# Three of the first four units by Strassen instead of two, with W2's sums made by accumulating DMAs

## Chip, cores and metric

One core of a Trainium2 chip runs the kernel. The metric is the device time in microseconds (us) of one execution. TensorE multiplies, VectorE and ScalarE do the elementwise work, GpSimd (POOL in the profile) a little of it, SyncE (SP) issues nearly all DMAs.

## What is computed

```python
B, N, V_DIM, Q_DIM = (64, 128, 1024, 512)      # x is (64, 128, 1024), all float32
q_emb = relu(cond_1024 @ W3 + b3)              # (64, 1024)
v_sum = sum(x, axis=1, keepdims=True)
y = (N * x + v_sum) * q_emb[:, None, :]
out = x + relu(y @ W2 + b2)                    # W2 is (1024, 1024)
```

Nearly all of the work is `y @ W2`: 8192 rows by 1024 by 1024, in an accuracy close to float32.

## The kernel before

**Units, quarters and the seven products.** Two sequences of `x` make a unit of 256 tokens, so there are 32 units, and two units make a pair: 16 pairs, 0 to 15. A unit is a 2 x 2 matrix of quarters A11, A12, A21, A22. The first index (t in the code) is the sequence, the second (h) the half of the 1024 features. A quarter lies in SBUF as 128 features by 4 tiles by 128 tokens (128 x 512 elements). W2 likewise has the quadrants b11, b12, b21, b22. A plain unit takes eight products of a quarter with a quadrant. By Strassen's method in Winograd's form a unit takes seven, named m = 1 to 7, in the order 1, 5, 6, 2, 7, 3, 4, with the two units c = 0, 1 of a pair alternating. Products 1, 2 and 4 use A11, A12 and A22 as they are, the others use sums of quarters. On W2's side the products use b11, b21, b22 and four sums t1 to t4 (OPERAND, line 54).

**Precision.** Each operand is split into a high part (a cast to fp32r, on ScalarE) and a low part (the difference, on VectorE). A product is 4 feature tiles by 3 matmuls of 512 columns (high by high, high by low, low by high), 12 matmuls into one of the 8 PSUM banks of `acc`. The parts of the tokens go through a ring of 7 places (`a_hi`, `a_lo`); a cast (`cast`, line 393, `cast_first`, 384) waits until the product that last read its place is done, and a product waits for the low part (`low`, 691, `low_first`, 686) by the semaphore `lo_ready`.

**Per unit, around the products.** VectorE sums the tokens (`token_sums`, 615) and makes scale and bias (`scalars`, 618). The tiles are then scaled in place, as a rule by ScalarE (`scale_quarter`, 406, four instructions a quarter), in the head also by VectorE and GpSimd. VectorE makes the sums of quarters (`sum_block`, 658). ScalarE seeds banks with the bias or with product 1 and saves the results of products 6 and 5 to SBUF tiles (`save_u2`, 473, `save_m5`, 464), because product 7 adds onto product 6's bank and product 3 onto product 5's; TensorE waits for these copies (lines 354 to 359). VectorE combines (`c22_sum`, `c12_sum`), applies relu and adds `x` (`result`, 705). SyncE loads and stores; a slot of `x_sb` (four units in all) is loaded again when the low part of the unit's product 4 is made (`load_pair`, 240).

**The head.** Pair 0 is multiplied plainly, 16 products (PLAIN_PRODUCTS, line 41), pair 1 is the first by Strassen (line 368), and a loop does the others (line 370). The token transform needs `q_emb`, so W3 comes first, staged in the `x_sb` slots of pair 1, whose tokens are loaded once its sums are taken (line 224). W2's quadrants are loaded once each, split in pieces (SPLIT, line 46; `cast_w`, `low_w`). The sums t1, t2 and t4 are made by VectorE in `w_stage` (`w_sum`, 702), t3 by GpSimd (line 611); for t4 b21 is loaded a second time (line 234).

**What sets the order.** Every engine has its own list of instructions, written out by hand in the code, and works it strictly in order; semaphores tie the lists together. An instruction whose wait isn't met holds up all that stand behind it on its engine. The lists of the head are lines 490 to 540 (ScalarE), 599 to 611 (GpSimd), 743 to 815 (VectorE) and 206 to 238 (SyncE); those of a pair are `pair` on ScalarE (542) and VectorE (817).

## Time and profile before

| | |
|---|---|
| median of 3 runs | 634.45 us (634.28 to 634.79) |
| the profiled execution | 634.83 us, span 633.0 us |
| TensorE busy | 628.6 us (99%), granted clock 1.00 |
| VectorE busy | 445.5 us (70%) |
| ScalarE busy | 419.0 us (66%) |
| GpSimd busy | 11.4 us (2%) |
| DMA | 108.83 MB, mean 172 GB/s |

The span runs from the first to the last instruction of the profiled execution; about 1.8 us of its time lie outside. Busy times are sums of instruction durations; on VectorE and ScalarE an instruction starts up to 0.1 us before the one ahead of it has ended, so a row's duration is longer than its share of a full list. A "releaser" is the instruction whose semaphore ended a wait.

### The profile page before, as it was taken

The numbers are of one execution on the slowest core, as the hardware profiler recorded it, in microseconds if no ns is written. First come the engines' busy times: TensorE is split into PE (matmuls) and PEld (weight loads), VectorE is DVE, ScalarE is ACT, GpSimd is POOL, SyncE is SP. The second block draws the span as 40 slices with busy tenths as digits, with TensorE's granted clock in tenths as the row PEclk, the third lists the DMA queues.
The fourth block names the chain that finished last, engine by engine and source line by source line (L and its number), as shares of the span: only waits on it lengthen the run. The fifth ranks groups of instructions, "written<-read, shape, count | busy, mean of one in ns | idle before, by whom it ended". The sixth has DMA issues, their size and how long they took to land.

```text
span 633.0 us, 9252 instructions
## 1 busy us (share of the span) xinstructions
PE 628.6 (99%) x2791; PEld 518.7 (82%) x2791; DVE 445.5 (70%) x683; ACT 419.0 (66%) x899; POOL 11.4 (2%) x14
## 2 busy tenths in 40 slices
PE   9999999999999999999999999999999999999997
PEld 6788888888888888888888888888888888888886
DVE  3899979675766757687576776757677576776533
ACT  4988886839476594856839577594856839577320
POOL 2130000000000000000000000000000000000000
PEclk9999999999999999999999999999999999999999
DMA  8925736564353734336354353744346354350703
GB/s 326 404 110 198 264 135 216 185 205 152 141 166 133 263 135 149 121 160 232 133 199 145 142 177 133 251 140 139 138 162 232 133 199 134 145 186 0 249 16 133
DMA packets 26654, 108.83 MB, mean 172 GB/s; under 512 B 2960, under 2 KB 3600, under 8 KB 22800
## 3 DMA queue, kind: packets, MB, share of 16 engines
q1 hardware_dynamic: 26208, 108.41, 48.3%
q10 hardware_dynamic: 432, 0.27, 0.2%
q8 instruction: 5, 0.08, 0.1%
q14 instruction: 9, 0.07, 0.0%
HBM read 75.11 MB, written 33.55 MB: 172 GB/s over the span
## 4 chain that ended last, share of the span: by engine, by line
PE 99%; DVE 0%; issue 0%; DVEq 0%
PE acc L293 99%; PE acc L310 1%; DVE xn L878 0%; DVE warm L743 0%; DVEq L57 0%
## 5 line engine op out<-in xcount | busy, mean ns | idle before, releaser
L293 PE MATMUL acc<-w_hi,a_hi 128*128 128x512 f32 x904 | 352.0, 389 | 0.0
L293 PE MATMUL acc<-w_lo,a_hi 128*128 128x512 f32 x904 | 351.7, 389 | 0.0
L293 PE MATMUL acc<-w_hi,a_lo 128*128 128x512 f32 x904 | 351.7, 389 | 0.0
L409 ACT ACTIVATE x_sb<-x_sb,bias,scale 128x128 f32<-128x128 f32 x492 | 203.2, 486 | 11.6 <-DVE bias L622 11.6
L293 PEld LDWEIGHTS acc<-w_hi,a_hi 128*128 128x128 f32 x904 | 169.7, 188 | 35.9 <-DVE a_lo L683 0.6
L293 PEld LDWEIGHTS acc<-w_hi,a_lo 128*128 128x128 f32 x904 | 169.7, 188 | 35.2
L293 PEld LDWEIGHTS acc<-w_lo,a_hi 128*128 128x128 f32 x904 | 169.7, 188 | 35.0
L694 DVE TENSOR_TENSOR a_lo<-x_sb,a_hi 128x512 fp32r<-128x512 f32 x150 | 103.5, 690 | 106.3 <-ACT a_hi L404 105.6
L404 ACT CAST a_hi<-x_sb 128x512 fp32r<-128x512 f32 x150 | 93.3, 622 | 38.6 <-PE acc L293 37.3
L404 ACT CAST a_hi<-s 128x512 fp32r<-128x512 f32 x60 | 37.4, 623 | 74.3 <-PE acc L293 69.1
L616 DVE TENSOR_REDUCE vsum<-x_sb 128x16 f32<-128x2048 f32 (+1 forms) x38 | 73.6, 1942 | 6.6 <-DMA x_sb<-x_t 6.6
L707 DVE SCALAR_TENSOR_TENSOR xn<-acc,xn 128x512 f32<-128x512 f32 x67 | 45.7, 689 | 32.6 <-PE acc L293 32.6
L462 ACT COPY acc<-acc 128x512 f32<-128x512 f32 x30 | 17.1, 571 | 49.1 <-PE acc L293 49.1
L694 DVE TENSOR_TENSOR a_lo<-s,a_hi 128x512 fp32r<-128x512 f32 x60 | 41.2, 687 | 0.2
L723 DVE TENSOR_TENSOR m_sb<-m_sb,acc 128x512 f32<-128x512 f32 x30 | 20.6, 687 | 23.0 <-PE acc L293 21.6
L733 DVE TENSOR_TENSOR u_sb<-u_sb,acc 128x512 f32<-128x512 f32 x30 | 20.6, 687 | 8.4 <-PE acc L293 8.4
L707 DVE SCALAR_TENSOR_TENSOR xn<-m_sb,xn 128x512 f32<-128x512 f32 x30 | 20.6, 685 | 0.2
L673 DVE TENSOR_TENSOR s<-s,x_sb 128x512 f32<-128x512 f32 x30 | 20.6, 686 | 0.1
L707 DVE SCALAR_TENSOR_TENSOR xn<-u_sb,xn 128x512 f32<-128x512 f32 x30 | 20.5, 685 | 0.1
L669 DVE TENSOR_TENSOR s<-x_sb 128x512 f32<-128x512 f32 x30 | 20.6, 685 | 0.0
L679 DVE TENSOR_TENSOR x_sb<-x_sb,s 128x512 f32<-128x512 f32 x30 | 20.5, 685 | 0.0
L675 DVE TENSOR_TENSOR x_sb<-x_sb 128x512 f32<-128x512 f32 x30 | 20.5, 685 | 0.0
(49 smaller groups left out, 189.3 us busy)
## 6 DMA issues: line engine op xcount, KB each, us to landing
xn<-x SPq DMA_DIRECT2D x64, 512.0 KB, 4.0
out<-xn SPq DMA_DIRECT2D x62, 512.0 KB, 3.3
x_sb<-x_t SPq DMA_DIRECT2D x30, 1024.0 KB, 5.4
x_sb<-w_t SPq DMA_DIRECT2D x4, 512.0 KB, 6.2
x_sb<-x_t SPq DMA_DIRECT2D x4, 512.0 KB, 10.7
u_sb<-w_q SPq DMA_DIRECT2D x3, 512.0 KB, 6.6
m_sb<-w_q SPq DMA_DIRECT2D x3, 512.0 KB, 6.5
out<-xn SPq DMA_DIRECT2D x3, 256.0 KB, 2.9
```

The source lines that it names most:

```text
L293: return nc.tensor.matmul(dst, lhs, rhs, start=False, stop=False, skip_group_check=True)
L404: nc.scalar.copy(a_hi[:, i % RING], operand(m, 2 * parity + c, c)).then_inc(hi_ready, 1)
L409: last = nc.scalar.activation(x_sb[:, slot, h, t, k], x_sb[:, slot, h, t, k], ACT.Identity, bias=bias[:, slot, h, t, k:k + 1], scale=scale ...
L616: nc.vector.tensor_reduce(sums, tokens, AX.X, ALU.add).then_inc(vsum_ready, 1)
L669: last = nc.vector.tensor_tensor(s, a21, a22, ALU.add)
L673: last = nc.vector.tensor_tensor(s, s, a11, ALU.subtract)
L675: last = nc.vector.tensor_tensor(a21, a11, a21, ALU.subtract)
L679: last = nc.vector.tensor_tensor(a12, a12, s, ALU.subtract)
L694: nc.vector.tensor_tensor(a_lo[:, i % RING], operand(m, 2 * parity + c, c), a_hi[:, i % RING].bitcast(fp32), ALU.subtract).then_inc(lo_rea ...
L707: nc.vector.scalar_tensor_tensor(o, bank, 0.0, o, ALU.max, ALU.add).then_inc(ready, 1)
L723: nc.vector.tensor_tensor(m5_sb[:, c], m5_sb[:, c], p_bank(parity, c), ALU.add).then_inc(c22_summed, 1)
L733: nc.vector.tensor_tensor(u2_sb[:, c], u2_sb[:, c], r_bank(c), ALU.add).then_inc(c12_summed, 1)
```

## The change

Only unit 0 is multiplied plainly (8 products). Unit 1 is done by Strassen together with units 2 and 3, 21 products, in one written list FIRST of 29; 14 of them come in a mixed early part, the other 15 in the list LATE. The loop over pairs 2 to 15 stays. In the new text m = 1 to 7 keep their meaning, `late(u, m)` is the place of a late operand among all operands made, and the products below are counted P0 to P28.

```diff
-    MADE = [((0, 0), 0, 4), ((1, 0), 0, 1), ((0, 0), 1, 2), ((1, 0), 1, 0),
-            ((0, 1), 0, 5), ((1, 1), 0, 3), ((0, 1), 1, 6), ((1, 1), 1, 4), ((0, 0), 0, 1)]
...
+    LATE = [(1, 5), (2, 5), (3, 5), (1, 3), (1, 6), (2, 3), (1, 7), (3, 3), (2, 6), (3, 6), (1, 4),
+            (2, 7), (3, 7), (2, 4), (3, 4)]
+    MADE = [(0, A11, 0), (0, A21, 1), (1, A11, 2), (2, A11, 3), (0, A12, 4), (0, A22, 5), (1, A12, 6), (2, A12, 2),
+            (3, A11, 3), (3, A12, 2)]
+    EARLY = len(MADE)
+    MADE += [(u, HOME[m], (j + 6) % RING) for j, (u, m) in enumerate(LATE)]
+    U1_BANK = {1: 0, 6: 0, 7: 0, 4: 0, 2: 5, 5: 1, 3: 1}
...
+    FIRST = [(0, "c11", 0, "b11", 3), (0, "c21", 1, "b11", 6), (1, 1, 2, "b11", 0), (2, 1, 3, "b11", 2),
+             (0, "c11", 4, "b21", 3), (0, "c21", 5, "b21", 6), (1, 2, 6, "b21", 5), (2, 2, 7, "b21", 4),
+             (0, "c12", 0, "b12", 1), (0, "c22", 1, "b12", 7), (3, 1, 8, "b11", 3),
+             (0, "c12", 4, "b22", 1), (0, "c22", 5, "b22", 7), (3, 2, 9, "b21", 5)]
+    FIRST += [(u, m, EARLY + j, OPERAND[m], late_bank(u, m)) for j, (u, m) in enumerate(LATE)]
```

W3 is staged in `xn`, the tile of the untransformed tokens, and the slots of units 2 and 3 are free for early loads. `s12` stays W2's stage throughout the head: the sums of quarters of units 1 to 3 are made in place, in quarters of `x_sb`, for which GpSimd takes A11 - A21 (`s3`) and the later sums and differences change sign.

```diff
-        w3_stage = x_sb[:, 2:4].rearrange("p s h t k n -> p (s h t k n)").rearrange("p (s t n) -> p s t n", s=KT, t=QT)
+        w3_stage = xn[:].rearrange("p c t d -> p (c t d)").rearrange("p (s t n) -> p s t n", s=KT, t=QT)
...
+        m5_u1, u2_u1 = u2_sb[:, 0], u2_sb[:, 1]
```

TensorE's waits for unit 1, and SyncE's loads and stores after the first ones:

```diff
+                if u == 1:
+                    if part == 2:
+                        pe.wait_ge(q_u1_seeded, 1)
+                    if part == 5:
+                        pe.wait_ge(r_u1_seeded, 1)
+                    if part == 3:
+                        pe.wait_ge(m5_u1_saved, 1)
+                    if part == 7:
+                        pe.wait_ge(u2_u1_saved, 1)
+                    if part == 4:
+                        pe.wait_ge(c22_u1_summed, 1)
...
+            sp.wait_ge(lo_ready, 6)
+            load_next(0)
+            store_first(0, 0, (c11_done, c12_done))
+            store_first(0, 1, (c22_done, c21_done))
+            for t in range(2):
+                sp.wait_ge(stored[0][t], 16)
+                load_xn(2, 0, t)
+            store_first(1, 0, (c11_done, c12_done))
+            sp.wait_ge(lo_ready, late(1, 4) + 1)
+            load_next(1)
```

ScalarE's list from the casts of t1 on (before it: `cast_first(4)`, `cast_first(5)`, `seed_q_u1()`, `scale_first(1, A12)`, casts 6 and 7, a seed, b12, two seeds, cast 8, b22, a seed):

```diff
+            for h in range(2):
+                cast_w("t1", h, t1_summed[h])
+            scale_first(3, A12)
+            cast_first(9)
+            scale_first(3, A22)
+            seed_q(1, 1, 1)
+            scale_first(2, A22)
+            cast_first(late(1, 5))
+            for h in range(2):
+                cast_w("t3", h, t3_summed[h])
+            act.wait_ge(b_step_ready, 1)
+            act.wait_ge(c12_done, 1)
+            nc.scalar.copy(acc[:, U1_BANK[5]], b_step[:]).then_inc(r_u1_seeded, 1)
+            act.wait_ge(c21_done, 1)
+            nc.scalar.copy(r_bank(0), b_step[:]).then_inc(r_seeded, 1)
+            cast_first(late(2, 5))
+            cast_w("t2", 0, t2_summed[0])
+            act.wait_ge(c22_done, 1)
+            nc.scalar.copy(r_bank(1), b_step[:]).then_inc(r_seeded, 1)
+            cast_first(late(3, 5))
+            cast_w("t2", 1, t2_summed[1])
+            save_m5_u1()
+            cast_first(late(1, 3))
+            cast_first(late(1, 6))
+            save_m5(1, 0)
+            cast_first(late(2, 3))
+            save_m5(1, 1)
+            cast_first(late(1, 7))
+            scale_usual(2, 0, 0)
+            cast_first(late(3, 3))
+            save_u2_u1()
+            cast_first(late(2, 6))
+            cast_first(late(3, 6))
+            for h in range(2):
+                cast_w("t4", h, t4_summed[h])
+            cast_first(late(1, 4))
+            scale_usual(2, 0, 1)
...
+            cast_first(late(3, 4))
+            save_u2(1, 1, 0)
+            scale_usual(2, 0, 3)
+            save_u2(1, 1, 1)
+            for n in (4, 5):
+                scale_usual(2, 0, n)
```

GpSimd's list. `add_half` is the accumulating DMA: the quadrant comes from HBM once more and is added to what lies in the stage, so t1 = b12 - b11 and its like become sums of the quadrants (the signs are taken up by the combinations).

```diff
+            def add_half(halves, kh, mh, h, summed):
+                half = slice(h * 2 * MH, (h + 1) * 2 * MH)
+                pool.dma_start(halves[h], w2_q[kh, mh, :, half], accum_op=ALU.add).then_inc(summed[h], 16)
...
+            scale_tiles(0, A11, range(2, KH))
+            scale_tiles(0, A21, range(KH // 2))
+            scale_tiles(0, A12, range(KH))
+            scale_tiles(0, A22, range(KH))
+            scale_tiles(2, A12, range(KH))
+            pool.wait_ge(w_lo_ready, split("b21", 1))
+            for h in range(2):
+                add_half(w_halves, 0, 1, h, t1_summed)
+            scale_tiles(3, A11, range(KH))
+            for h in range(2):
+                pool.wait_ge(w_lo_ready, split("b12", h))
+                add_half(v_halves, 1, 1, h, t3_summed)
+            pool.wait_ge(b_seeded, len(SEEDED))
+            nc.gpsimd.tensor_tensor(b_step[:], b_step[:], b_first[:], ALU.add).then_inc(b_step_ready, 1)
+            scale_tiles(1, A21, range(KH))
+            s3(1)
+            scale_tiles(1, A22, range(KH))
+            for h in range(2):
+                pool.wait_ge(w_lo_ready, split("t1", h))
+                add_half(w_halves, 1, 1, h, t2_summed)
+            scale_tiles(2, A21, range(KH))
+            s3(2)
+            scale_tiles(3, A21, range(KH))
+            s3(3)
+            for h in range(2):
+                pool.wait_ge(w_lo_ready, split("t2", h))
+                add_half(w_halves, 1, 0, h, t4_summed)
```

VectorE's list, after the b11 low parts (`stats` is the sums and scalars of one quarter, both quarters of a half for (3, A12)):

```diff
+            low_first(3)
+            low_w("b21", 0)
+            stats(1, A12)
+            low_first(4)
+            low_w("b21", 1)
...
+            first_result(0, "c12", 0, 0, 1, c12_done)
+            stats(2, A22)
+            low_first(late(1, 5))
+            first_result(0, "c21", 0, 1, 0, c21_done)
+            stats(3, A21)
+            sum_first(2, 5)
+            first_result(0, "c22", 0, 1, 1, c22_done)
+            low_first(late(2, 5))
+            sum_first(3, 5)
+            sum_first(1, 6)
+            low_first(late(3, 5))
+            sum_first(1, 3)
+            low_w("t3", 0)
+            low_first(late(1, 3))
+            low_w("t3", 1)
+            low_first(late(1, 6))
+            for h in range(2):
+                low_w("t2", h)
+            sum_first(2, 6)
+            sum_first(2, 3)
+            low_first(late(2, 3))
+            low_first(late(1, 7))
+            sum_first(3, 6)
+            sum_first(3, 3)
+            sums_usual(0, 0, x_loaded[0], 16)
+            scalars_usual(2, 0, 0)
+            low_first(late(3, 3))
+            c12_u1()
+            low_first(late(2, 6))
+            low_first(late(3, 6))
+            c22_u1()
+            for h in range(2):
+                low_w("t4", h)
+            low_first(late(1, 4))
+            low_first(late(2, 7))
+            low_first(late(3, 7))
+            sums_usual(0, 1, x_loaded[1], 16)
+            scalars_usual(2, 0, 1)
+            low_first(late(2, 4))
+            low_first(late(3, 4))
```

## Rows read from the trace of the kernel before

**Rows 1.** Page, part 1: busy us of each engine, share of the span, instructions.
```profile
PE 628.6 (99%) x2791; PEld 518.7 (82%) x2791; DVE 445.5 (70%) x683; ACT 419.0 (66%) x899; POOL 11.4 (2%) x14
```

**Rows 2.** Chain that ended last, in order of time: start us, us, what.
```profile
12.55 617.28 PE acc L293 x2728
```

**Rows 3.** Waits of the whole run: engine, line, releaser: us in total, times, longest.
```profile
PEld acc L293 <- DVE a_lo L683: 0.6, 2, 0.4
```

**Rows 4.** Timeline, TensorE's weight loads: start us, us, what, idle before and releaser.
```profile
17.35 0.19 PEld L293 LDWEIGHTS acc<-w_hi,a_hi 128*128 128x128 f32 x1 [0.43 <-DVE a_lo L683]
25.69 0.19 PEld L293 LDWEIGHTS acc<-w_hi,a_hi 128*128 128x128 f32 x1 [0.19 <-DVE a_lo L683]
```

**Rows 5.** Timeline, VectorE, 23 to 28 and 70 to 73 us.
```profile
23.47 1.23 DVE L699 TENSOR_TENSOR w_lo<-u_sb,w_hi 128x1024 fp32r<-128x1024 f32 x1 [0.74 <-ACT w_hi L437]
...
24.95 0.69 DVE L683 TENSOR_TENSOR a_lo<-x_sb,a_hi 128x512 fp32r<-128x512 f32 x1 [0.24 <-ACT a_hi L391]
25.55 1.22 DVE L699 TENSOR_TENSOR w_lo<-m_sb,w_hi 128x1024 fp32r<-128x1024 f32 x1
26.69 0.68 DVE L616 TENSOR_REDUCE vsum<-x_sb 128x4 f32<-128x512 f32 x1
...
27.48 0.68 DVE L683 TENSOR_TENSOR a_lo<-x_sb,a_hi 128x512 fp32r<-128x512 f32 x1
...
70.58 2.28 DVE L616 TENSOR_REDUCE vsum<-x_sb 128x16 f32<-128x2048 f32 x1
...
72.98 0.69 DVE L675 TENSOR_TENSOR x_sb<-x_sb 128x512 f32<-128x512 f32 x1
```

**Rows 6.** Timeline, ScalarE, at 36 and from 73 to 77 us.
```profile
36.55 2.01 ACT L437 CAST w_hi<-w_stage 128x1024 fp32r<-128x1024 f32 x2
...
73.10 1.65 ACT L409 ACTIVATE x_sb<-x_sb,bias,scale 128x128 f32<-128x128 f32 x4 [1.52 <-DVE bias L622]
74.66 0.57 ACT L479 COPY u_sb<-acc 128x512 f32<-128x512 f32 x1
75.12 0.62 ACT L404 CAST a_hi<-x_sb 128x512 fp32r<-128x512 f32 x1
75.64 1.66 ACT L409 ACTIVATE x_sb<-x_sb,bias,scale 128x128 f32<-128x128 f32 x4
```

**Rows 7.** Timeline, GpSimd, looked at one instruction at a time.
```profile
13.29 1.76 POOL L594 TENSOR_SCALAR x_sb<-x_sb,scale,bias 128x128 f32<-128x128 f32 x1 [0.18 <-DVE bias L622]
15.04 0.87 POOL L594 TENSOR_SCALAR x_sb<-x_sb,scale,bias 128x128 f32<-128x128 f32 x1
20.87 0.45 POOL L594 TENSOR_SCALAR x_sb<-x_sb,scale,bias 128x128 f32<-128x128 f32 x1 [4.96 <-DVE bias L622]
38.56 2.40 POOL L611 TENSOR_TENSOR w_extra<-m_sb,w_extra 128x1024 f32<-128x1024 f32 x1
```

**Rows 8.** Page, part 6, DMA issues: count, KB each, median us to landing.
```profile
x_sb<-x_t SPq DMA_DIRECT2D x30, 1024.0 KB, 5.4
...
s<-w_q SPq DMA_DIRECT2D x1, 512.0 KB, 15.5
```

**Rows 9.** Timeline, VectorE, beside GpSimd's work.
```profile
14.21 1.39 DVE L699 TENSOR_TENSOR w_lo<-w_stage,w_hi 128x512 fp32r<-128x512 f32 x2
...
20.69 0.68 DVE L616 TENSOR_REDUCE vsum<-x_sb 128x4 f32<-128x512 f32 x1
...
22.00 0.73 DVE L683 TENSOR_TENSOR a_lo<-x_sb,a_hi 128x512 fp32r<-128x512 f32 x1 [0.42 <-ACT a_hi L391]
...
40.34 0.65 DVE L620 TENSOR_SCALAR scale<-q_emb 128x16 f32<-128x16 f32 x1
```

**Rows 10.** Timeline, SyncE's queue: the issue of half a W2 quadrant.
```profile
24.73 0.33 SPq L194 DMA_DIRECT2D u_sb<-w_q  x1
```

More of the change, by code:

```diff
@@ L339, in _, with product @@
                 last.then_inc(prod_done, 1)
-            def product(p, parity, i, first=False):
+            for n in range(len(FIRST)):
+                first_product(n)
+            def product(p, parity, i):
                 m, c = ORDER[i]
@@ L366, in product @@
                 last.then_inc(prod_done, 1)
-            for i in range(STEPS):
-                product(1, 1, i, first=True)
             with nc.Fori(0, (PAIRS - 2) // 2, engines=(mybir.EngineType.PE,), hint_back_edge=True) as l:
@@ new lines, in cast_first_part, with cast_first @@
+                nc.scalar.copy(a_hi[:, place, part], quarter(u, q)[:, part]).then_inc((hi_started, hi_ready)[h], 1)
+            def cast_first(o):
+                u, q, place = MADE[o]
+                if o < EARLY:
+                    act.wait_ge(x0_scaled[u, q], 2 if o == 1 else 1)
+                else:
+                    m = LATE[o - EARLY][1]
+                    if m == 4:
+                        act.wait_ge(x0_scaled[u, A22], 1)
+                    elif m == 7:
+                        act.wait_ge(s3_ready, u)
+                    else:
+                        act.wait_ge(sum_ready, FIRST_SUMS.index((u, m)) + 1)
+                old = [n for n, (_, _, other, _, _) in enumerate(FIRST) if other < o and MADE[other][2] == place]
@@ new lines, in scale_tiles, with s3 @@
+                last.then_inc(x0_scaled[u, q], 1)
+            def add_half(halves, kh, mh, h, summed):
+                half = slice(h * 2 * MH, (h + 1) * 2 * MH)
+                pool.dma_start(halves[h], w2_q[kh, mh, :, half], accum_op=ALU.add).then_inc(summed[h], 16)
+            def s3(u):
+                pool.wait_ge(lo_ready, [v == u and q == A11 for v, q, _ in MADE].index(True) + 1)
+                pool.wait_ge(x0_scaled[u, A21], 1)
+                nc.gpsimd.tensor_tensor(quarter(u, A11), quarter(u, A11), quarter(u, A21), ALU.subtract).then_inc(s3_ready, 1)
@@ L678, in sum_block @@
                     dve.wait_ge(sum_ready, summed(p, ORDER.index((6, c))))
-                    last = nc.vector.tensor_tensor(a12, a12, s, ALU.subtract)
+                    last = nc.vector.tensor_tensor(a12, a12, s, ALU.add)
                 last.then_inc(sum_ready, 1)
```

493 lines of the change are left out of this document (258 added, 235 removed), and 3 rows, old and new, of the table PLAIN_PRODUCTS.

## Prediction, made before the changed kernel was run

> **What bounds the kernel now.** I read the busy times first [rows 1]: TensorE works for 99% of the span. The chain that ended last, in order of time [rows 2], is one unbroken piece of its matmuls, 617.28 us from 12.55 to 629.83. So time is gained only by giving it fewer matmuls, and lost wherever it has to wait. Third, the waits [rows 3]: TensorE's weight loads waited for another engine twice, 0.6 us in all, and the timeline gives both [rows 4]: 0.43 at 17.35, before the second product, and 0.19 at 25.69, before the fifth. So the 225 products from 17.35 on take (629.83 - 17.35 - 0.19) / 225 = 2.721 us each. VectorE and ScalarE have average slack (70% and 66%), but what they must deliver before each product in the first 100 us decides here.
>
> **What the change removes.** Before: 16 products for the plain pair and 15 x 14 for the others, 226. After: 8 for unit 0, 7 each for units 1 to 3, 14 x 14 for the rest, 225. One product less: **-2.72 us**. The loop over the later pairs keeps its instructions; signs change between add and subtract on the same tiles, at no cost. W3 moves to the space of the token tile: the four loads keep their queue places, and what follows (token tiles now, unit 2 and 3 before) waited for the same sums. The q-sums, the first product and its operands keep their order. I cost these at nothing.
>
> **What it adds, by product.** P0 to P28 are the new products of units 0 to 3; P_n is due at 17.35 + 2.721 (n - 1) plus the waits so far. Each engine works its list in order, so I add the lists up from rows. Pitches (start to start, back to back): VectorE 0.60 for a 512-element operation, 1.13 for 1024, 0.60 + 0.20 for one quarter's sums and scalars, 2.2 + 0.2 for a whole unit's [rows 5]. ScalarE 1.55 for four scaled tiles, 0.46 for a copy into SBUF, 0.52 for a cast, 0.95 for a W2 cast of 1024 [rows 6]. The receiver starts at the end of the full duration (0.69, 1.65, 0.57, 0.62, 1.05) plus about 0.05.
>
> P4 (due 25.51). Before, the low part of its tokens ran at 24.95. Now the sums of (unit 1, A12) stand between it and the W2 low part that started at 23.47 [rows 5]: 23.47 + 1.13 + 0.80 = 25.40, ready at 26.1. TensorE waits 0.6 instead of 0.19: **+0.4**.
>
> P14 (unit 1, m = 5). P11 ends at 17.35 + 11 x 2.721 + 0.6 = 47.9; VectorE takes its result (0.60), then the sums for (2, A22) (0.80), which release ScalarE's four tiles at 49.65. Behind them are a cast (0.52), two W2 casts for t3 (1.90) and only then the bias seed that P14 waits for (0.58): 49.65 + 1.55 + 0.52 + 1.90 + 0.58 + 0.05 = 54.25, against a due time of 53.35: **+0.9**.
>
> P19 (unit 2, m = 3): by the list that the next part adds up, VectorE makes its sum at 66.1, behind the t2 low parts and another sum. Sum, cast and low part in full are 0.74 + 0.67 + 0.74 with the hand-overs, so 68.3, and P19 is due at 67.9: **+0.4**.
>
> P20 (unit 1, m = 7), the largest term. It adds onto the bank of P18, so it waits until ScalarE has saved P18, and that copy is queued behind four tiles of unit 4 and a cast. The tiles need unit 4's scalars, which VectorE makes after a long list. From the end of P11 (48.1 on VectorE): 18 operations of 512, two sums with scalars, four W2 low parts, one unit's sums: 10.8 + 1.6 + 4.5 + 2.4 = 19.3 us of work. Idle inside it: 2.3 (the low part of P14 waits for the four tiles and the cast above), 1.1 (sum (3, m = 5) waits for GpSimd: scalars at 53.9, four tiles at 0.45, a 512 subtraction at 1.2, half of the 1024 one [rows 7]), and 2.0 in six short round trips to ScalarE. 48.1 + 19.3 + 5.4 = 72.8; then 0.1 + 1.55 + 0.52 + 0.57 + 0.05 gives 75.7. P20 is due at 71.0: **+4.7**. Before, ScalarE waited 1.52 at its like place [rows 6], but the save behind it was ready at 75.2 and its product due at 17.35 + 23 x 2.721 = 79.9.
>
> P26 and P27. Unit 5 cannot be loaded until unit 1 has left its slot. P20 ends at 78.4; VectorE's two operations (1.3), two t4 low parts (2.26) and the low part of (1, m = 4) end at 82.9. The 1 MB load takes 5.4 [rows 8], sums and scalars 2.4, ScalarE's four tiles and the save behind them 2.2: 93.2, and P26 is due at 92.0: **+1.2**. ScalarE then has eight more tiles (3.1) and a cast (0.6), VectorE a low part and the difference that P27 waits for (1.3 + 0.1): 98.1 against 95.9, **+2.2**.
>
> GpSimd. Its 8 scaled tiles become 36, with three 512 subtractions, a bias sum and eight accumulating DMAs in place of two 1024 subtractions. Beside a VectorE reduction (20.69) a tile took 0.45; beside a dense run of operations with both operands in SBUF (the pair at 14.21 is its end) one took 1.76 and the next 0.87, and VectorE's small scalar operation at 40.34 lasted 0.65, until GpSimd's subtraction had ended [rows 7, 9]. Each can hold the other up. On the chain above GpSimd has the four tiles of (3, A21) and one subtraction; of VectorE's work beside them two operations have both operands in SBUF, some 0.6 each. I take **+1.0**; the ends are 0 (all at 0.45) and 5.1 (every tile at 0.87, as at 15.04, and every subtraction at 1.8, lengthened by one 0.60 operation). The Trainium skill, "SBUF — State Buffer", section "Who interferes with whom", has the loser blocked for the full instruction: by that rule the sum would go to the upper end, 646.6, and this trace agrees only in part: the tile of 1.76 waited out more than one operation, but the low part at 22.00, begun beside a tile, took 0.73 against the usual 0.69 [rows 9].
>
> The accumulating DMAs: no row shows one. Issue: bounded by SP's 0.33 for such a half [rows 10] and GpSimd's own 2.40 for a tile of that size [rows 7]; I take 1.0, nearer the row that is an issue. At 0.33 the sum stays, at 2.40 P14 waits 1.0 more. Landing: between 5.4 for 1 MB in a quiet stretch and 15.5 for 512 KB in the crowded start [rows 8]. Up to 8 us all eight are covered (t1 is issued at 30 and needed at 38, t2 at 44 for 55, t3 at 34 for 52, t4 at 64 for 76), so they cost nothing; at 12 they cost 2, at 16 some 12. I take 5, near the quiet row, since most are issued after the crowded start. The Trainium skill, "DMA: Bandwidth & Descriptors", section "Anatomy of one DMA", gives about 2.0 us plus the bytes at 436 GB/s, an estimate of 3.2 us, which would leave the sum as it is. In exchange VectorE loses six 1024 subtractions, 6.8 us, already left out of its lists above.
>
> **Sum.** 0.4 + 0.9 + 0.4 + 4.7 + 1.2 + 2.2 + 1.0 = 10.8 of new waits, less 2.72: +8.1. Against the profiled execution (634.83 around a span of 633.0) 642.9; against the median of 634.45, which lies 0.4 below it, **642.5 us**. From P29 on both engines have their former lists, at 70% and 66% busy [rows 1], so I expect nothing further.
>
> **The rivals.** *The feeding keeps pace* (faster). The only gain is the product, so 634.45 - 2.72 = 631.7. It needs the 5.4 us of VectorE's idle before P20 to be absent, since the work alone would have ScalarE's copy ready at 70.3, and unit 5 landed some 3 us earlier than a 5.4 us load gives. For it: the work does fit. Against it: the 2.3 and 1.1 follow from queue order with durations of 690 and 1650 ns that hardly vary. It turns to a gain below 2.7 us of waits. 12%.
>
> *GpSimd becomes the bound* (slower still). It lies in the contention of [rows 7, 9]: with tiles at 0.87 and subtractions at 1.8 the new waits are 14.9 (P14 2.6, P16 2.6, P19 0.9, P5 0.35, the rest as above) and the time 646.6; if an issue also costs 2.40, P14 alone waits 7 and P15 2.8, and the time is 655. It decides once GpSimd's list from 28 on slips by 4 us, its margin at 45.9 before sum (1, m = 5). For it: 24 tiles from 28 to 56, VectorE's fullest stretch. Against: many VectorE operations there are reductions or read PSUM, and beside a reduction the tile took 0.45. 15%.
>
> *A part of the waits falls away*: loads landing after 3.5 us take out 2, no contention 1: 639.5; I hold this inside the forecast.
>
> **Chances.** Forecast 70% (639 to 646), GpSimd bound 15%, feeding keeps pace 12%, something between that ends within 0.2% (1.3 us, about what a measurement of this kernel can tell from no change) 3%. So faster 0.12, same 0.03, slower 0.85. The range 637 to 649 leaves out the gain and the upper part of the GpSimd case, together under 2 in 10.
>
> **What the profile would show.** Right: one break of 4 to 5 us in TensorE between 70 and 77, released by a copy of ScalarE into the u2 tile; ScalarE's tile group before it waiting for VectorE's scalars; a VectorE reduction waiting 4 to 5 us for the token load near 84; breaks of 1 to 2 us near 93 and 98; 2700 matmuls of 512 float columns instead of 2712, and no waits later. Wrong: TensorE's waits in the first 100 us under 3 us in all, or the greatest one before P14 or P16, released through GpSimd.

## The result, and the profile after it

The changed kernel took **651.28 us** (median of 6 executions, 649.89 to 652.42) against 634.58 us for the kernel before on the same chip: ratio 1.0264, 95% interval 1.0254 to 1.0274. That is 16.7 us slower; 8.1 were forecast, and the value lies 2.3 us above the range. The profiled execution took 652.42 us, with a span of 650.3.

The page of the changed kernel, parts 1 (busy us, share, instructions), 2 (the span in 40 slices: the granted clock in tenths) and 5 (operation, count | busy us, mean ns | idle before it, releaser):

```profile
PE 631.9 (97%) x2779; PEld 519.1 (80%) x2779; DVE 445.7 (69%) x692; ACT 411.4 (63%) x878; POOL 39.8 (6%) x52
...
PEclk9997988999999999999999999999999999999999
...
L354 PE MATMUL acc<-w_hi,a_hi 128*128 128x512 f32 x900 | 353.6, 393 | 13.8 <-issue 10.0
...
L721 POOL TENSOR_SCALAR x_sb<-x_sb,scale,bias 128x128 f32<-128x128 f32 x36 | 29.0, 1045 | 20.9 <-DVE bias L772 20.9
```

Against [rows 1], TensorE has 12 matmuls fewer, and its share fell from 99% to 97%: it stood idle 13.8 us before matmuls of this kind. In slices 4, 6 and 7, all within the first 115 us, its clock was not fully granted. GpSimd's busy time went from 11.4 to 39.8 us; a record of one tile lasted 1045 ns on the mean (records overlap: the 36 tiles kept it busy for 29.0 us, 0.81 each).

The last piece of the chain that ended last (start us, us, what) is unbroken, so no wait came later, as forecast:

```profile
106.50 540.47 PE acc L354 x2376
```

It holds P27 and everything behind it and ends at 646.97; [rows 2] ended at 629.83. So 17.14 us have to be found ahead of 110 us. TensorE's breaks are in its timeline (start us, us, instruction, idle before it and releaser):

```profile
17.04 0.50 PE L354 MATMUL acc<-w_hi,a_hi 128*128 128x512 f32 x1 [0.30 <-DVE a_lo L844]
25.87 0.50 PE L354 MATMUL acc<-w_hi,a_hi 128*128 128x512 f32 x1 [0.35 <-DVE a_lo L844]
50.87 0.50 PE L354 MATMUL acc<-w_hi,a_hi 128*128 128x512 f32 x1 [0.18 <-DVE a_lo L844]
59.47 0.77 PE L354 MATMUL acc<-w_hi,a_hi 128*128 128x512 f32 x1 [5.57 <-issue]
82.09 0.77 PE L354 MATMUL acc<-w_hi,a_hi 128*128 128x512 f32 x1 [4.47 <-issue]
101.57 0.47 PE L354 MATMUL acc<-w_hi,a_hi 128*128 128x512 f32 x1 [0.77 <-ACT u_sb L567]
106.50 0.47 PE L354 MATMUL acc<-w_hi,a_hi 128*128 128x512 f32 x1 [1.97 <-DVE m_sb L913]
```

From 25.87 on these are P4, P13, P14, P20, P26 and P27. P14's break is 5.57 us where 0.9 was forecast. And after long breaks the products themselves are slow: the windows (busy us and matmuls of TensorE, granted clock, DMA share, GB/s) show the clock at its lower level, 1.2 instead of 2.4 GHz:

```profile
50.00:55.00 5.00, 3.73 (x16) 1.00 0.22 20
...
56.00:62.00 6.00, 2.53 (x6) 0.50 0.98 263
62.00:63.00 1.00, 1.00 (x4) 0.63 0.92 262
63.00:68.00 5.00, 5.00 (x24) 1.00 0.61 197
...
80.00:86.00 6.00, 3.91 (x9) 0.50 0.23 90
...
107.00:110.00 3.00, 3.00 (x9) 0.52 1.00 422
```

P14 to P19 took 18.15 us from 59.47 to the end of P19 (82.09 less 4.47) instead of 6 x 2.721 = 16.33: 1.8 lost. In the same way P20 to P25 lost 2.4 (101.57 - 0.77 - 82.09 = 18.71), and the last piece, 198 products, 540.47 - 538.76 = 1.7. Summed: idle 0.35 + 0.18 + 5.57 + 4.47 + 0.77 + 1.97 = 13.3, slow products 5.9, less the product saved (2.72), less 0.3 because P1 starts at 17.04 instead of 17.35, less the 0.19 that the kernel before waited too [rows 4]: 16.0 of 17.14. The other 1.2 is in pieces of 0.2 to 0.3 between the starts printed (P1 to P4, P4 to P13, P13 to P14, P26 to P27), for which the timeline names no wait.

**Behind P14.** GpSimd's timeline:

```profile
31.80 4.35 POOL L721 TENSOR_SCALAR x_sb<-x_sb,scale,bias 128x128 f32<-128x128 f32 x4
35.74 1.25 POOL L727 DMA_DIRECT2D s<-w_q  x1
40.67 0.89 POOL L727 DMA_DIRECT2D w_extra<-w_q  x1 [3.68 <-issue]
41.23 1.64 POOL L748 TENSOR_TENSOR b_step<-b_step,b_first 128x512 f32<-128x512 f32 x1
42.51 6.17 POOL L721 TENSOR_SCALAR x_sb<-x_sb,scale,bias 128x128 f32<-128x128 f32 x4
48.83 1.29 POOL L733 TENSOR_TENSOR x_sb<-x_sb 128x512 f32<-128x512 f32 x1 [0.15 <-POOL x_sb L721]
50.11 2.24 POOL L721 TENSOR_SCALAR x_sb<-x_sb,scale,bias 128x128 f32<-128x128 f32 x4
```

The last line is the four tiles of (1,A22), needed for the sum (1,5). Two things stand out: four tiles took 4.35 and 6.17 us where 1.8 (0.45 each) were forecast, and the fourth accumulating DMA came 3.68 us late with no releaser. VectorE's timeline carries the delay on,

```profile
41.49 1.48 DVE L770 TENSOR_SCALAR scale<-q_emb 128x8 f32<-128x8 f32 x1
...
52.45 0.69 DVE L858 TENSOR_TENSOR x_sb<-x_sb 128x512 f32<-128x512 f32 x1 [1.63 <-POOL x_sb L721]
```

and ScalarE's:

```profile
45.02 1.05 ACT L529 CAST w_hi<-w_stage 128x1024 fp32r<-128x1024 f32 x1 [3.54 <-DMA w_stage<-w_q]
...
54.84 1.65 ACT L502 ACTIVATE x_sb<-x_sb,bias,scale 128x128 f32<-128x128 f32 x4 [4.52 <-DVE bias L772]
...
58.79 0.58 ACT L649 COPY acc<-b_step 128x512 f32<-128x512 f32 x1
```

The sum (1,5) waits for GpSimd; behind it on VectorE stand a result and the scalars of (2,A22), behind those on ScalarE four tiles, a cast, two casts of t3, and then the copy of b_step into P14's bank, ready at 59.37. The second half of t1 was cast at 45.02, though its DMA was issued by 32.4. So there were several candidates: the gap on GpSimd, its slow tiles, the late t1, and the order of ScalarE's list. The experiments separate them.

**Behind P20** the profile agrees with the forecast chain, ScalarE's timeline:

```profile
79.36 1.65 ACT L502 ACTIVATE x_sb<-x_sb,bias,scale 128x128 f32<-128x128 f32 x4 [4.56 <-DVE bias L772]
80.91 0.60 ACT L488 CAST a_hi<-x_sb 128x512 fp32r<-128x512 f32 x1
81.42 0.58 ACT L581 COPY u_sb<-acc 128x512 f32<-128x512 f32 x1
```

### The profile page after: what moved, and what is told of

It is laid out like the page before. It is cut to its first block, busy times and chain, and to the rows that moved or that the text cites. A ratio compares the mean times of both kernels' runs of the same rounds, so it can differ in the third digit from the quotient of the medians.

```text
span 650.3 us, 9176 instructions
## 1 busy us (share of the span) xinstructions
PE 631.9 (97%) x2779; PEld 519.1 (80%) x2779; DVE 445.7 (69%) x692; ACT 411.4 (63%) x878; POOL 39.8 (6%) x52
## 4 chain that ended last, share of the span: by engine, by line
PE 87%; POOL 3%; DVE 3%; DMA 2%; ACT 2%; issue 2%; SPq 0%; DVEq 0%; ACTq 0%; POOLq 0%
PE acc L354 87%; POOL x_sb L721 2%; DMA w_stage<-w_q 1%; ACT x_sb L502 1%; DMA x_sb<-x_t 1%; DVE w_lo L877 1%; DVE vsum L766 1%; DVE a_lo L844 0%; ACT a_hi L488 0%; ACT w_hi L529 0%; POOL w_stage L727 0%; SPq L231 0%; DVE xn L882 0%; POOL b_step L748 0%; POOL x_sb L733 0%
## 5 line engine op out<-in xcount | busy, mean ns | idle before, releaser
L354 PE MATMUL acc<-w_hi,a_hi 128*128 128x512 f32 x900 | 353.6, 393 | 13.8 <-issue 10.0
L354 PEld LDWEIGHTS acc<-w_hi,a_hi 128*128 128x128 f32 x900 | 170.2, 189 | 52.4 <-issue 12.2
L502 ACT ACTIVATE x_sb<-x_sb,bias,scale 128x128 f32<-128x128 f32 x468 | 193.3, 486 | 22.6 <-DVE bias L772 22.6
L872 DVE TENSOR_TENSOR a_lo<-x_sb,a_hi 128x512 fp32r<-128x512 f32 x140 | 96.7, 690 | 105.9 <-ACT a_hi L497 105.4
L497 ACT CAST a_hi<-x_sb 128x512 fp32r<-128x512 f32 x140 | 87.1, 622 | 37.6 <-PE acc L354 36.1
L766 DVE TENSOR_REDUCE vsum<-x_sb 128x16 f32<-128x2048 f32 (+2 forms) x43 | 74.4, 1733 | 10.9 <-DMA x_sb<-x_t 10.9
L497 ACT CAST a_hi<-s 128x512 fp32r<-128x512 f32 x56 | 34.8, 622 | 72.8 <-PE acc L354 69.1
L872 DVE TENSOR_TENSOR a_lo<-s,a_hi 128x512 fp32r<-128x512 f32 x56 | 38.5, 688 | 0.4
L721 POOL TENSOR_SCALAR x_sb<-x_sb,scale,bias 128x128 f32<-128x128 f32 x36 | 29.0, 1045 | 20.9 <-DVE bias L772 20.9
L923 DVE TENSOR_TENSOR u_sb<-acc,u_sb 128x512 f32<-128x512 f32 x30 | 20.7, 691 | 8.4 <-PE acc L354 8.4
L844 DVE TENSOR_TENSOR a_lo<-x_sb,a_hi 128x512 fp32r<-128x512 f32 (+2 forms) x26 | 17.5, 685 | 9.0 <-ACT a_hi L488 8.6
L488 ACT CAST a_hi<-x_sb 128x512 fp32r<-128x512 f32 x24 | 14.4, 618 | 12.7 <-DVE x_sb L866 5.5
L567 ACT COPY u_sb<-acc 128x512 f32<-128x512 f32 x30 | 17.4, 580 | 5.4 <-PE acc L354 5.3
## 6 DMA issues: line engine op xcount, KB each, us to landing
x_sb<-x_t SPq DMA_DIRECT2D x7, 512.0 KB, 11.4
```

The lines of the kernel that those rows point to most:

```text
L354: return nc.tensor.matmul(dst, lhs, rhs, start=False, stop=False, skip_group_check=True)
L497: nc.scalar.copy(a_hi[:, i % RING], operand(m, 2 * parity + c, c)).then_inc(hi_ready, 1)
L502: last = nc.scalar.activation(x_sb[:, slot, h, t, k], x_sb[:, slot, h, t, k], ACT.Identity, bias=bias[:, slot, h, t, k:k + 1], scale=scale ...
L567: nc.scalar.copy(u2_sb[:, c], p_bank(parity, c)).then_inc(u2_saved, 1)
L721: last = nc.gpsimd.tensor_scalar(x_sb[:, u, h, t, k], x_sb[:, u, h, t, k], scale[:, u, h, t, k:k + 1], bias[:, u, h, t, k:k + 1], ALU.mult ...
L766: nc.vector.tensor_reduce(sums, tokens, AX.X, ALU.add).then_inc(vsum_ready, 1)
```

## The experiments

Each was timed beside the kernel before, whose medians were 634.0 to 634.8 us. Times are medians; "less" and "more" are against the change's 651.28 or the run named. Runs 1 to 4, 5 to 8, 9 to 11 and 12 are four groups, each with its own timing of the kernel before, so a small difference between groups is judged by the ratios.

**1. The descriptor space of GpSimd's DMAs.**

```diff
-    nc = bacc.Bacc("TRN2", target_bir_lowering=False, num_devices=1, dynamic_dma_scratch_size=1024)
+    nc = bacc.Bacc("TRN2", target_bir_lowering=False, num_devices=1, dynamic_dma_scratch_size=2048)
```

```profile
36.36 1.60 POOL L727 DMA_DIRECT2D w_extra<-w_q  x1
36.92 2.36 POOL L748 TENSOR_TENSOR b_step<-b_step,b_first 128x512 f32<-128x512 f32 x1
```

The gap before the fourth DMA is gone, and with it the wait of the sum (1,5) for GpSimd (it ran at 49.52). P14 came at 56.60 after 3.17 us instead of 5.57. So the stall was one of descriptor space; 3.2 us of P14's wait have another cause. Its tiles stayed slow (four took 4.37 and four 5.78).

**2. Unit 1's eight tiles from GpSimd to ScalarE**, with the small descriptor space.

```diff
-            scale_tiles(1, A21, range(KH))
             s3(1)
-            scale_tiles(1, A22, range(KH))
...
+            scale_first(1, A21)
             act.wait_ge(c11_done, 1)
             nc.scalar.copy(p_bank(1, 1), b_first[:]).then_inc(p_seeded, 1)
-            for h in range(2):
-                cast_w("t1", h, t1_summed[h])
+            cast_w("t1", 0, t1_summed[0])
+            scale_first(1, A22)
+            cast_w("t1", 1, t1_summed[1])
```

> The eight scaled tiles of unit 1's A21 and A22 go from GpSimd to ScalarE (beside the casts of t1), nothing else. Theory A, GpSimd's list is what holds P14: VectorE's wait before sum (1, m = 5) goes (1.6), its two small scalar operations of 1.48 and 1.17 shrink to about 0.2, and the wait before P14 falls from 5.9 to 2 to 4; if it falls below some 2.5 the half clock after it goes as well (1.7 more). The time falls by 2 to 5. Rival C, P14 is held by the late landing of t1's second half (ScalarE waits until 45.0 for it): VectorE's low part of t1 stays at 46 to 48.4 and the time falls by 1.6 at most.

Measured: 648.98 us, ratio 1.0234 (1.0217 to 1.0251); P14 at 57.05 after 3.63. Another way round the same late link, with the same result as 1: the sum (1,5) no longer waits for GpSimd, and over 3 us stay. GpSimd still touches the path: of VectorE's two small operations, expected at 0.2, one fell from 1.17 to 0.15 us, the other grew from 1.48 to 2.35, over an addition and a subtraction of GpSimd.

**3. The save that P20 waits for, ahead of unit 4's tiles.**

```diff
-            scale_usual(2, 0, 0)
             cast_first(late(3, 3))
             save_u2_u1()
+            scale_usual(2, 0, 0)
```

> On ScalarE the four scaled tiles of unit 4 go behind the save of P18 and the cast before it, nothing else. The forecast's step: P20's wait of 4.6 is the queue order; it falls to under 1, the half clock after it (82 to 86.7, worth 2.3) goes too, and the waits before P26 and P27 stay as they are. The time falls by 5 to 7. Rival: VectorE's list is late in any case, so that P21 or P22 takes over the wait and the time falls by less than 2.

Measured: 645.65 us, ratio 1.0172 (1.0152 to 1.0191), 5.6 less than the change by moving one line. P20 has no break any more, the clock stays at 1.00 from 64 to 100 us, and P26 gave back 1.3 (2.05 instead of 0.77). No work was taken away.

**4. The clock.** Matmuls of zeros, 22 ahead of P14 and 18 ahead of P20, fill the idle time. They add onto bank 2 and so change no value.

```diff
             for n in range(len(FIRST)):
+                for _ in range({14: 22, 20: 18}.get(n, 0)):
+                    keep_warm()
                 first_product(n)
```

> TensorE gets 22 matmuls of 512 columns of zeros (bf16, added onto bank 2) before P14 and 18 before P20, where it waits 5.9 and 4.6 us; they change no value. If the half clock after these two waits follows from the idleness: it goes in both places, the time falls by some 4 us (1.7 and 2.3), and the waits end where they ended. Rival: the clock falls for another reason (the work of the head as such): it falls as before and the time stays within 0.5 us, or gets longer by the part of the filling that does not fit.

Measured: 648.47 us, ratio 1.022 (1.0203 to 1.0237), 2.8 less. The windows show the clock whole up to 100 us:

```profile
50.00:60.00 10.00, 9.12 (x41) 1.00 0.66 140
60.00:70.00 10.00, 9.70 (x43) 1.00 0.51 176
...
80.00:90.00 10.00, 9.39 (x42) 1.00 0.13 52
```

P20 still started at 81.86 (82.09 in the change): the 1.8 us that P14 to P19 could have gained went into new waits for VectorE's low parts (0.30 at P16, 0.67 at P19), pieces for which the timeline names no wait, and P20's own gap (4.67 us from the end of P19, filling included, instead of 4.47). Only the clock after P20 was worth something at the end, about its 2.4 us. So the clock's fall is a consequence of TensorE's idleness, and a real cost only where no later wait swallows it.

**5. Both edits, 1 and 3**, with no other line changed, as the base of what follows.

> The 2048-byte scratch and the later tiles of unit 4 together. If the two causes are independent: P14's wait near 3.2 as with the scratch alone, none before P20, and the gains add (2.5 and 5.6): about 643. Rival, they overlap, because what P14 gives back is waited for again behind VectorE's list before P20: about 645.

Measured: 643.63 us, ratio 1.0139 (1.012 to 1.0158). TensorE's timeline:

```profile
56.89 0.47 PE L354 MATMUL acc<-w_hi,a_hi 128*128 128x512 f32 x1 [3.08 <-issue]
75.58 0.47 PE L354 MATMUL acc<-w_hi,a_hi 128*128 128x512 f32 x1 [0.46 <-issue]
94.19 0.47 PE L354 MATMUL acc<-w_hi,a_hi 128*128 128x512 f32 x1 [2.01 <-ACT u_sb L567]
99.13 0.69 PE L354 MATMUL acc<-w_hi,a_hi 128*128 128x512 f32 x1 [1.93 <-DVE m_sb L913]
```

P14, P20, P26, P27. The two edits nearly add up: 2.5 + 5.6 = 8.1 against 7.65 measured.

**6. Unit 4's load later**, on 5, so that it does not cross the accumulating DMAs of t1.

```diff
-            sp.wait_ge(lo_ready, 6)
+            sp.wait_ge(lo_ready, 10)
             load_next(0)
```

> As the run before, and SyncE issues the 1 MB load of unit 4 (not needed before 72) some 20 us later, out of the crowded stretch in which t1 is fetched. Theory D, t1's second half lands late because the DMA queues are crowded: it lands 2 us or more earlier than at 44.8, ScalarE's wait of 2.5 before its cast goes, P14's wait falls by 1 to 2. Rival: the accumulating DMA is slow by itself; the landing stays within 0.5.

Measured: 643.72 us, ratio 1.0137 (1.0114 to 1.0161). The cast of t1's second half came at 43.46 instead of 44.84, so the transfers do hold one another up. But P14 stayed at 57.11 after 3.01. VectorE's timeline tells why: it is back to back from 37.44 to 52.4, whenever t1 lands (three of its lines, and the cast ahead of the first on ScalarE):

```profile
36.79 0.62 ACT L488 CAST a_hi<-x_sb 128x512 fp32r<-128x512 f32 x1 [1.55 <-POOL x_sb L721]
...
37.44 0.69 DVE L844 TENSOR_TENSOR a_lo<-x_sb,a_hi 128x512 fp32r<-128x512 f32 x1 [1.72 <-ACT a_hi L488]
...
38.65 1.21 DVE L770 TENSOR_SCALAR scale<-q_emb 128x4 f32<-128x4 f32 x1
...
50.65 0.69 DVE L882 SCALAR_TENSOR_TENSOR xn<-acc,xn 128x512 f32<-128x512 f32 x1
```

The last is the result (0,c12), which could have run at 48.66, when P11 ended in this run: it is 2.0 us late (2.1 in 1 and in 5). The first two lines show how much of that is GpSimd's. Its four tiles of (3,A11) took 4.34 us, so the cast came 1.55 later and the full stretch began later by as much; and the operation at 38.65 lasted 1.21 instead of 0.16. Together 2.6, more than the 2.0. Read so, the list by itself would have been in time; no run makes these tiles elsewhere, so this is not shown by experiment.

**7. Edits 1, 2 and 3 together.**

> As the first of this group, and unit 1's eight tiles on ScalarE instead of GpSimd. If GpSimd's list still holds P14 once the scratch is doubled: P14's wait falls from about 3.2 to 2 or less. Rival: with the scratch doubled VectorE no longer waits for GpSimd before sum (1, m = 5), so nothing more is gained: within 0.5 us of the first run of this group.

Measured: 643.45 us, ratio 1.014 (1.0121 to 1.0158), the same as 5. P14's wait was 3.63, P27's fell to 0.35. Once its DMAs do not stall, taking these tiles off GpSimd brings P14 nothing.

**8. The order at P26 and P27**, on 5: the first save ahead of unit 5's tiles, and the subtraction for P27 ahead of the usual loop.

```diff
-            scale_usual(2, 0, 3)
             save_u2(1, 1, 1)
-            for n in (4, 5):
+            for n in (3, 4, 5):
...
+            low_first(late(2, 4))
+            low_first(late(3, 4))
+            c11(1, 0)
             sums_usual(0, 1, x_loaded[1], 16)
             scalars_usual(2, 0, 1)
-            low_first(late(2, 4))
-            low_first(late(3, 4))
-            c11(1, 0)
             first_result(1, 4, 1, 1, 0, c21_done)
+            c22_sum(1, 1, 0)
...
```

> As the first of this group, and unit 5's part reordered: ScalarE saves P23 ahead of unit 5's tiles, VectorE makes the last two low parts ahead of unit 5's sums, and the difference that P27 waits for directly after them. The forecast's step for P26 and P27: both waits (2.1 and 2.0 where P20 no longer waited) go to under 0.3 and so does the half clock near 101; the time falls by 4 to 5.5 against the first run. Rival: the load of unit 5 comes so late that P29 or P30 takes the wait over; the time falls by less than 2.

Measured: 643.94 us, ratio 1.015 (1.0132 to 1.0168): a miss. TensorE's timeline:

```profile
100.61 0.64 PE L354 MATMUL acc<-w_hi,a_hi 128*128 128x512 f32 x1 [3.75 <-DVE m_sb L912]
```

Two waits of 2 became one of 3.75, at P28, one product behind P27: P28 waits for the like subtraction of unit 3, still behind low parts that wait for ScalarE's casts behind unit 5's tiles. A wait is gone only if all that share its list are moved.

**9. The order at P14**, on 5. On ScalarE:

```diff
-            scale_first(2, A22)
             cast_first(late(1, 5))
-            for h in range(2):
-                cast_w("t3", h, t3_summed[h])
             act.wait_ge(b_step_ready, 1)
             act.wait_ge(c12_done, 1)
             nc.scalar.copy(acc[:, U1_BANK[5]], b_step[:]).then_inc(r_u1_seeded, 1)
+            scale_first(2, A22)
...
```

The casts of t3 follow around that of (2,5), both of t2 behind that of (3,5). VectorE makes the low part of P13 ahead of the scalars of (2,A21), and the low part of (1,5) and the scalars of (2,A22) and (3,A21) ahead of the result of c21.

> The larger descriptor scratch and the save of unit 1's product six ahead of unit 4's tiles, as before (643.6 us), and now the lists around P14 alone are put in another order. ScalarE: the cast of (1,5) and the copy of b_step into its bank before the four tiles of (2,A22) and before the casts of t3. VectorE: the scalars of (2,A22) and (3,A21) ahead of the results of unit 0. The same instructions in all. Theory (order): what is left of P14's wait, 3.1 us, is ScalarE's copy into the bank standing behind four tiles (1.65) and two casts of t3 (1.9) that P14 does not need, and they in turn behind VectorE's scalars. Then P14 has its bank near 52 to 53 us instead of 56.8, before P13 has ended near 53.7, and its wait goes. Every later product is due 3 us sooner: of the 3.1 us some returns as waits at P15, P16 or P20. I expect 641.0 (640.3 to 642.5) and at P14 under 0.7. Rival (late data): P14 waits for t1's second half or for GpSimd's tiles whatever the order, then its wait stays over 2 us and the time is 643.0 to 644.0. Rival (moved on): P14's wait goes and as much comes at P15 or P16, whose tiles GpSimd makes: time again 643 to 644, with a wait of 2 us or more there.

Measured: 641.61 us, ratio 1.0121 (1.0104 to 1.0138). P14 has no wait any more; P15 has one:

```profile
57.82 0.50 PE L354 MATMUL acc<-w_hi,a_hi 128*128 128x512 f32 x1 [2.19 <-DVE a_lo L844]
```

So another order of these two lists is enough to free P14. Of its 3.08 us, 2.19 moved on to the next product, as the second rival had it. About 0.9 of them is GpSimd's: the low part that P15 waits for lasted 1.59 us instead of 0.69, beside the subtraction of unit 3. P27's wait fell from 1.93 to 0.44; P26's stayed (2.02). The time is the theory's, but against 5 the intervals of the ratios overlap (the medians differ by 2.0, the ratios by 1.1 us); in the profiled executions P27 started at 96.61 instead of 99.13.

**10. Both ends in order**: 7 and 9, and the end of the first stretch with both subtractions ahead of the loop and the casts of units 4 and 5 between the tiles.

```diff
-            scale_usual(2, 0, 3)
             save_u2(1, 1, 1)
-            for n in (4, 5):
-                scale_usual(2, 0, n)
...
                     cast(p, parity, i)
-                    if i < 2:
+                    if isinstance(p, int) and p == 2:
+                        if i < 5:
+                            scale_usual(p, parity, 3 + i)
+                    elif i < 2:
                         scale_usual(p, parity, 6 + i)
...
             first_result(1, 4, 1, 1, 0, c21_done)
+            for c in range(2):
+                c22_sum(1, 1, c)
...
```

> The order around P14 of the run before this one, unit 1's eight tiles by ScalarE instead of GpSimd, and the end of the first stretch in another order too: both of VectorE's subtractions that P27 and P28 wait for before the low parts of the usual loop, ScalarE's casts of the loop's first two operands between the tiles of units 4 and 5 and not behind them. The same instructions in all. Theory (order): every wait of TensorE in the first 110 us was one of order, not of work, so with both ends in order few are left: P14, P20, P26, P27 and P28 together under 3 us. The floor is the kernel before less one product, 634.5 - 2.7 = 631.8; I expect 635.5 (633.5 to 638.5). Rival (work): VectorE and ScalarE are full up to product 28, so a wait taken away at one product comes back at a later one, and the sum of the waits from P14 on stays above 5 us: 638.5 to 641.5.

Measured: **637.67 us**, ratio 1.005 (1.0034 to 1.0067): 13.6 us of the change's 16.7 are gone with the same work, by order, descriptor space and eight tiles on the other engine. All breaks of TensorE behind the first product's:

```profile
26.11 0.50 PE L354 MATMUL acc<-w_hi,a_hi 128*128 128x512 f32 x1 [0.29 <-DVE a_lo L844]
59.32 0.50 PE L354 MATMUL acc<-w_hi,a_hi 128*128 128x512 f32 x1 [2.77 <-DVE a_lo L844]
70.99 0.50 PE L354 MATMUL acc<-w_hi,a_hi 128*128 128x512 f32 x1 [0.50 <-DVE a_lo L844]
74.57 0.47 PE L354 MATMUL acc<-w_hi,a_hi 128*128 128x512 f32 x1 [0.53 <-issue]
```

None at P26 to P28. Of the five products that the theory had named only P20 waits (0.53), but it had not named P15 (2.77) and P19 (0.50). From P14 on 3.8 us of waits are left, less than the 5 of the rival, and the time lies within the theory's range. P15 is again held by a low part that lasted as long as GpSimd let it:

```profile
57.66 1.60 DVE L844 TENSOR_TENSOR a_lo<-x_sb,a_hi 128x512 fp32r<-128x512 f32 x1 [0.95 <-ACT a_hi L488]
```

**11. t1 by VectorE again**, on 5: one part of the change undone.

```diff
-            for h in range(2):
-                add_half(w_halves, 0, 1, h, t1_summed)
...
             for h in range(2):
+                dve.wait_ge(b12_loaded[h], 16)
+                nc.vector.tensor_tensor(w_halves[h], w_halves[h], v_halves[h], ALU.add).then_inc(t1_summed[h], 16)
                 low_w("b12", h)
```

> The larger descriptor scratch and the earlier save, as before (643.6 us), and t1 (b11 + b12) is summed by VectorE in two additions of 128x1024 (about 1.2 us each) instead of by GpSimd's two accumulating DMAs: one part of the change undone. Theory (lists): the DMAs, slow as they land (9 to 14 us), are covered once the scratch holds; VectorE's list is what holds P14, so it is held 2.4 us longer there: P14's wait 5 to 6 us instead of 3.1, and the clock's fall is longer again; 646.0 (645.0 to 647.5). Rival (transfers): it is the late landing of t1's second half (cast at 44.8, low parts at 47 to 49) that sets VectorE's pace up to P14, then the additions cost nothing, the wait stays or shrinks, and the time is 642.0 to 643.8.

Measured: 645.7 us, ratio 1.0171 (1.0152 to 1.0189), 2.1 more than 5 (the intervals of the two ratios just touch). The time is the theory's, P14's wait is not (5 to 6 expected): P14 came at 58.06 after 3.83, and an earlier product waited 1.07 at 42.99. VectorE's timeline shows one of its low parts held fast:

```profile
37.05 3.04 DVE L841 TENSOR_TENSOR a_lo<-x_sb,a_hi 128x512 fp32r<-128x512 f32 x1 [0.85 <-ACT a_hi L488]
```

So giving t1's sums to DMAs is worth some 2 us, once the descriptor space holds them.

**12. More scalars ahead of P14**, on 10: VectorE makes those of (2,A21) ahead of t1's low parts and those of (3,A21) ahead of unit 0's result, and GpSimd makes the tiles of (2,A21) before it issues t2's DMAs.

```diff
+            stats(2, A21)
             for h in range(2):
                 low_w("t1", h)
-            stats(2, A21)
             low_first(9)
             sum_first(1, 5)
+            stats(2, A22)
+            stats(3, A21)
             first_result(0, "c12", 0, 0, 1, c12_done)
-            stats(2, A22)
             low_first(late(1, 5))
             first_result(0, "c21", 0, 1, 0, c21_done)
-            stats(3, A21)
```

> The kernel with both ends in order (637.7 us), with one more reordering for its largest wait, 2.77 us at P15 (59.32): there ScalarE's cast of (2,5) came at 57.02 and VectorE's low part was held to 59.3 by GpSimd's subtraction s3 of unit 3. Now VectorE makes the scalars of (2,A21) ahead of t1's low parts, those of (2,A22) and (3,A21) ahead of unit 0's result and of P14's low part, and GpSimd makes the four tiles of (2,A21) and their s3 before the two DMAs of t2. The same instructions in all. Theory (order, to the end): P14 is then due 0.6 us late (its low part at 54.3 instead of 52.5, P13 ends at 53.8), P15 and P16 no more than 0.5 late each, so that of 2.77 some 1.2 to 1.6 are left: 636.3 (635.3 to 637.0), still slower than the kernel before. Rival (work): VectorE is full from 37 to 57 us, so the 1.7 us of scalars put ahead of P14 come back whole at P14 or P16: 637.3 to 638.5. Rival (order was all): all waits of this stretch go, 635.0 or below.

Measured: 639.38 us, ratio 1.0081 (1.0067 to 1.0095): a miss, slower than 10 and than all three numbers expected. GpSimd's timeline:

```profile
47.45 4.66 POOL L723 TENSOR_SCALAR x_sb<-x_sb,scale,bias 128x128 f32<-128x128 f32 x4 [5.12 <-DVE bias L772]
52.26 1.31 POOL L735 TENSOR_TENSOR x_sb<-x_sb 128x512 f32<-128x512 f32 x1
```

VectorE's:

```profile
52.38 1.21 DVE L772 TENSOR_TENSOR bias<-vsum,q_emb 128x4 f32<-128x4 f32 x1
```

Four tiles beside VectorE's low parts took 4.66 us (2.64 in 10, after them), and the 0.15 us operation at 52.38 lasted as long as GpSimd's subtraction. P14 and P15 waited 1.6 each, and t2, issued some 5 us later, kept ScalarE waiting 2.02 at 63.73 and made a new wait of 1.27 for P17, whose cast stood behind it. None of the three numbers expected had a price for tiles that are slowed in this way.

## Why the prediction was wrong, step by step

The sign and the cause were right: TensorE is fed late in the first stretch, at the places named. Term by term, forecast and found:

- P20, +4.7, and 1.0 more for GpSimd on its chain, 5.7: 4.47 at 82.09, through the chain named, and 3 shows that the order of one save is all of it. The chain itself was well sized: from P14's start to P20's 22.45 were forecast (the 1.0 included) and 22.62 measured, and VectorE's wait for GpSimd in it was 2.13 instead of 1.1. The wait came out near 4.7 by luck: the products between took 18.15 instead of 16.75, by the clock, and hid that much of the chain.
- P4, +0.4 (0.6 of wait): 0.35 at 25.87. P27, +2.2: 1.97. P26, +1.2: 0.77. P19, +0.4: nothing, since P14's late start had made it due later. One product less, -2.72: the matmuls are 2700 instead of 2712.
- **P14, +0.9: the step that failed.** It was 5.6 idle. The working took VectorE to be free at P11's end (47.9) for its result and started adding there. It had not added up the list ahead of that: in 6, where neither t1 nor a stall is late, that list is back to back from 37.44 and reaches the result at 50.65, 2.0 us after P11's end. With the 0.9 of the forecast that is about the 3.0 that P14 waits there. The other 2.4 are the stall of GpSimd's fourth DMA (1), through the sum (1,5). What makes the list late is open in part: by 6's trace it is GpSimd, by 9 another order is enough.
- **The GpSimd term, +1.0**, was put on its four tiles of (3,A21), where it held, and the upper end used 0.87 a tile. But it was missing ahead of P14. In VectorE's dense stretch a tile took 1.09 and 1.54 (4.35 and 6.17 for four), and GpSimd in turn made 0.15 us operations of VectorE last 1.2 to 1.5. The rival "GpSimd becomes the bound" named this place and its margin of 4 us before the sum (1,5), and the margin was used up: the tiles due by 49.9 ended at 52.35. Without the stall they ended at 48.45 (1), so slow tiles alone did not use it up. It had 15% and priced the time at 646.6. That the accumulating DMAs could stall GpSimd's queue was in neither case. One of the forecast's own signs of being wrong did come: the greatest wait stood before P14, 2.4 us of it through GpSimd.
- **Accumulating DMAs.** Issue, taken at 1.0 between 0.33 and 2.40: 0.83 to 1.25. Landing, taken at 5 between 5.4 and 15.5: 5.3 to 13.8, median 9.2. The late t1 looked guilty on ScalarE (3.54 of wait) and was not: bringing it forward changed nothing at P14 (6), and summing it on VectorE was worse (11). With room for the descriptors, "covered" was right.
- **The clock: left out.** The sum priced each wait at its idle time. The products behind the three long ones lost 5.9 us more. Of that the filling in 4 recovered 2.8.
- Three sums of the working do not come out as printed: VectorE's release before P14 is 47.9 + 0.60 + 0.80 = 49.3 without hand-overs, not 49.65; unit 5's save is 82.9 + 5.4 + 2.4 + 2.2 = 92.9, not 93.2; and the upper case of the GpSimd rival, P14 at 7 instead of 2.6 and 2.8 at P15, gives 653.8, not 655. None of them decides.

The Trainium skill, "SBUF — State Buffer", section "Who interferes with whom", has the loser blocked for the full instruction. By that rule I would have gone to 646.6, and VectorE's held operations here (1.17 to 1.48 instead of 0.15, about one GpSimd instruction each) bear it out better than the rows of before did; the one of 2.35 in 2 outlasted two. The Trainium skill, "DMA: Bandwidth & Descriptors", section "Anatomy of one DMA", by which I gave an estimate of 3.2 us for 512 KB, is contradicted for these transfers: none landed under 5.3.

What 10 still pays against the kernel before: its span is 3.0 us longer. Its waits are 3.5 us more (4.1 against the 0.6 of [rows 3]), less 2.7 for the product; from P4's start at 26.11 to P31's at 104.74 the 27 products took 1.4 us more than 2.721 each and their waits, in pieces of 0.2 to 0.5 for which the timeline names no wait. That and a start of P4 later by 0.3 than its wait explains makes 2.5. The other 0.5, and what lengthens the products by those pieces, stays open. Staging W3 in xn was not tried by itself; P1 started 0.3 earlier and nothing ahead of it was longer.

## What to carry to other kernels

When a change starves the engine that bounds, add up the whole list of each feeding engine from where it was last idle, not from the event that it is thought to wait for, and price what a neighbour can lengthen in it; here the ten back-to-back microseconds ahead of the first "due" time held 2.0 us of error, and a stall on GpSimd 2.4. Then, before giving work away, look at what stands in front of the one copy that the bounding engine waits for: moving four scaled tiles behind one save was worth 5.6 us, and order with room for the descriptors 13.6 of 16.7, while a reordering that moved only one of several waiters gained nothing (8) and one that crowded two engines lost (12). Price an idle stretch of TensorE of several microseconds above its length, unless a later wait swallows the difference.
